# Two transformer layers on one core: the keys' transposition, a feed-forward product and its GELU move to other slots, two products change bank, and the routing bias is added in groups

## The chip, the core and the metric

The kernel runs on one core of a Trainium2 chip. A core has four compute engines that the text calls by the profile's names: PE (TensorE, matrix products; PEld is its weight load), DVE (VectorE), ACT (ScalarE) and POOL (GpSimd), and a queue engine SP that only starts transfers. Each engine executes its own list of instructions strictly in the order in which they were written; they wait for each other through semaphores. PE writes its results into eight PSUM banks, from which ACT and DVE read them. The metric is the device time of one execution in microseconds, the median over runs.

## The reference

Inputs are `x` (16 batches of 128 tokens, 128 wide) and a context of 77 tokens for each batch. Two layers follow each other:

```
x = x + tanh(g_xattn[0]) * L0_xattn(ctx, layernorm(x))   # 16 heads of 64, 77 context + 128 latent keys, masked softmax
x = x + tanh(g_ffn[0])   * L0_ffn(layernorm(x))          # 128 -> 512, butterfly, gelu, butterfly, 512 -> 128
x = x + tanh(g_xattn[1]) * L1_xattn(layernorm(x), ctx)   # 16 heads of 8, softmax over the 32 largest of 77 scores
x = x + tanh(g_ffn[1])   * L1_ffn(layernorm(x))          # router, one of 8 experts for each token
```

with, in the last of them,

```
route = sigmoid(x @ Wr + br)
max_prob, max_ind = max(route), argmax(route)
out = gelu(x @ W1[max_ind]) @ W2[max_ind] * max_prob
```

The 32 largest scores are found with four rounds of "the eight largest" and "replace them" for each head; this is the bulk of DVE's work.

## The kernel before

**Staging.** The 16 batches go through a software pipeline in `run_steps`. In a step `i` six batches are in the works: `P = i` (its keys are being normalised), `A = i-1` (first attention), `A2 = i-2` (end of the first attention, first feed-forward product), `B = i-3` (second feed-forward product, scores of the second attention), `C = i-4` (the 32 largest, softmax) and `E = i-5` (end of the second attention, router). Steps 0 to 5 and 16 to 20 are written out; steps 6 to 15 are one loop body that runs ten times. A step has eight slots; each engine has a function `step` that lists, slot by slot, what it issues. That list alone sets the order: there is no planner. After the last step the tokens are sorted by expert and the expert products run (the last 68 us); nothing in that stage is touched.

**The banks.** The eight banks are `GZ`, `S0`, `S1`, `TC`, `TL`, `OA`, `X`, `M`. `S0` and `S1` hold the first attention's scores, `TC` and `TL` its transposed probabilities, `GZ` and `OA` take turns for the projections, `X` holds 512-wide products (first feed-forward product, second attention's scores and transposed probabilities), and `M` everything small. Before PE writes a bank again it waits, in `free(name)`, for the semaphore of the last reader of that bank.

**The work around the change.** `keys_T` turns the normalised context and latents into bank `M`; `keys_out` on ACT copies them to `kvT`, which every projection of the batch needs. `queries_in`, `keys_in` and `values_in` are these projections; `queries_kept`, `keys_kept` and `values_kept` their copies on ACT; `scores(b, q)` are the scores of four heads; `maxima` on DVE the row maxima of two heads each; `exps(b, p)` the exponentials of two heads on ACT, which wait for the maxima; `normalise` on POOL, `probs_T` on PE, `probs_out` on ACT and `attend` on PE follow. `hidden` is the first feed-forward product (L892), `gelus` its activation on ACT (L1183, output `f_h`), `down` the second product (L900). `logits` is the router's product (L964), 8 columns wide. ACT needs another function table for Gelu than for Exp: the compiler puts an `ACT_TABLE_LOAD` in front of the first instruction that needs the other table. `top_32(b, k)` on DVE works on two heads; 8 of them belong to a batch.

In slot 0 before the change PE issues `keys_T(A)`, `attend(A2, GZ, 2)`, `down(B)` into `M`, the queries, the keys and `scores(A, 0)`; in slot 6 `hidden(A2)`; ACT issues `keys_out(A)` first in slot 0 and `gelus(A2)` in slot 6, ahead of `exps(A, 6)`; DVE adds the router's bias in slot 7 straight from bank `M`, and the residual of `down(B)` at the start of slot 0.

## Time and profile before

| | us |
|---|---|
| median of 3 runs | 811.86 (810.77 to 813.05) |
| the profiled execution | 816.19 |
| its span, from first to last instruction | 814.50 |
| PE busy in the span | 671.9 |
| DVE busy | 563.6 |
| ACT busy | 484.5 |
| POOL busy | 448.6 |
| ten passes of the loop body | 396.93 |

The span can be cut at the copy of `kvT` on ACT, of which there is one in each step. The steps from the sixth copy on (217.82 us) are alike in their work: 276 matmul records, 31.4 us of DVE and 28.3 us of ACT each. Their lengths are not all alike: in the ten loop passes there are lengths of about 38.7 and of about 40.3 us. The rows below come from one short and one long pass, and from the last step.

### The profile page before, as it was taken

What the parts mean: (1) busy time and instruction counts of PE and PEld (TensorE: products, weight loads), DVE (VectorE), ACT (ScalarE), POOL (GpSimd) and SP (SyncE); (2) the same over time, 40 slices, a digit from 0 to 9 for tenths busy, and PEclk for the clock granted to TensorE, in tenths of its full rate; (3) what the DMA queues carried; (4) which work ended last, traced back from release to release, by engine and by line L of the source; (5) the groups of instructions that cost most, each with busy time, mean ns of one, the idle gap of its engine ahead of it and who ended that gap; (6) DMA issues with size and microseconds to landing.
All of it is one profiled execution on the core that took longest, in us unless ns stands there. A gap on an engine that the chain in (4) does not pass through costs nothing.

```text
span 814.5 us, 19311 instructions
## 1 busy us (share of the span) xinstructions
PE 671.9 (82%) x4994; PEld 538.8 (66%) x4994; DVE 563.6 (69%) x3753; ACT 484.5 (59%) x1315; POOL 448.6 (55%) x689
## 2 busy tenths in 40 slices
PE   5498977889898989898989898989898968854696
PEld 4466665767676767667676767777767656543696
DVE  3266415778796969786868787878787889994232
ACT  1166558586767777777776776767776744221231
POOL 6445737565665646473737473737465553753144
PEclk9789999999999999999999999999999985555798
DMA  7200199900000000000000000000000000100672
GB/s 192 60 1 1 37 307 314 304 24 1 2 2 1 0 0 0 0 0 0 0 0 0 0 0 0 0 0 0 0 0 2 1 2 1 40 33 33 194 230 78
DMA packets 38535, 37.88 MB, mean 47 GB/s; under 512 B 3633, under 2 KB 34249, under 8 KB 38484
## 3 DMA queue, kind: packets, MB, share of 16 engines
q1 hardware_dynamic: 32986, 27.76, 12.0%
q10 hardware_dynamic: 3994, 6.36, 2.9%
q0 software_dynamic: 1504, 3.17, 1.1%
q8 instruction: 22, 0.36, 0.2%
q14 instruction: 29, 0.24, 0.1%
HBM read 16.28 MB, written 21.45 MB: 46 GB/s over the span
## 4 chain that ended last, share of the span: by engine, by line
PE 33%; ACT 21%; DVE 15%; issue 13%; POOL 11%; SPq 3%; DMA 2%; POOLq 1%; another core or an unknown queue 0%; DVEq 0%; ACTq 0%
DVE sw L1554 5%; ACT L1183 5%; PE bank L714 4%; ACT prob L1183 4%; PE bank L802 4%; DVE m L1548 4%; ACT sw L1183 3%; PE score_banks L844 3%; PE bank L900 3%; PE bank L1155 3%; POOL second_keys L496 3%; PE bank L814 3%; PE bank L1165 3%; PE bank L868 2%; PE bank L824 2%
## 5 line engine op out<-in xcount | busy, mean ns | idle before, releaser
L1554 DVE MATCH_REPLACE8 sw<-m,sw 128x77 f32<-128x77 f32 x1024 | 220.2, 222 | 0.0
L1548 DVE MAX8 m<-sw 128x8 f32<-128x77 f32 x1024 | 189.3, 226 | 8.7 <-DVE sw L1554 5.1
L1183 ACT ACTIVATE prob<-score_banks,negmax 128x205 f32<-128x205 f32 x256 | 108.2, 433 | 50.2 <-DVE negmax L1496 50.1
L503 POOL TENSOR_TENSOR sw<-sw,m 128x616 f32<-128x616 f32 x64 | 78.0, 1218 | 95.2 <-DVEq L1530 95.1
L484 POOL TENSOR_TENSOR prob<-prob,inv 128x820 f32<-128x820 f32 x64 | 99.4, 1554 | 50.6 <-DVE inv L1501 50.6
L1496 DVE TENSOR_REDUCE negmax<-score_banks 128x2 f32<-128x410 f32 x128 | 68.5, 577 | 62.1 <-PE score_banks L844 62.1
L937 PEld LDWEIGHTS bank<-v,p1T 77*128 77x128 f32 x512 | 73.8, 217 | 34.6 <-issue 20.6
L937 PE MATMUL bank<-v,p1T 77*128 (+1 forms) x512 | 74.5, 273 | 17.2 <-DVE rows_out L1508 12.6
L1554 DVE MATCH_VALUE_LOAD sw<-m,sw 128x8 f32 x1024 | 77.9, 76 | 0.0
L714 PEld LDWEIGHTS bank<-ident,prob 128*77 128x77 f32 (+1 forms) x512 | 57.5, 147 | 19.2 <-issue 18.8
L868 PE MATMUL bank<-ptc,z_ring 77*64 77x128 f32 x512 | 53.5, 284 | 20.0 <-ACT z_ring L1183 18.4
L714 PE MATMUL bank<-ident,prob 128*77 128x128 f32 (+1 forms) x512 | 68.0, 276 | 0.0
L824 PE MATMUL bank<-raw,kvT 128*128 128x512 f32 (+1 forms) x128 | 66.5, 602 | 0.0
L1183 ACT ACTIVATE h_ring<-bank 128x256 f32<-128x256 f32 (+1 forms) x87 | 38.6, 443 | 45.8 <-PE bank L1155 33.0
L1183 ACT ACTIVATE z_ring<-bank 77x512 f32<-77x512 f32 x64 | 38.1, 596 | 44.7 <-PE bank L824 44.6
L814 PE MATMUL bank<-kvT,raw 128*128 128x205 f32 x256 | 58.5, 353 | 0.8 <-ACT z_ring L1183 0.8
L844 PE MATMUL score_banks<-k_sb,q_sb 64*128 64x205 f32 x512 | 59.1, 348 | 0.0
L920 PE MATMUL bank<-second_keys,b_q 128*128 128x308 f32 x128 | 52.6, 495 | 4.7 <-ACT p1T L1183 4.7
L868 PEld LDWEIGHTS bank<-ptc,z_ring 77*64 77x64 f32 x512 | 29.9, 135 | 39.2 <-issue 39.1
L510 POOL TENSOR_TENSOR p<-sw 128x308 f32<-128x308 f32 x64 | 46.9, 733 | 15.8 <-ACT sw L1183 15.7
L1183 ACT ACT_TABLE_LOAD x34 | 43.6, 1283 | 19.8 <-issue 17.4
L1183 ACT ACTIVATE sw<-bank 128x308 f32<-128x308 f32 x64 | 28.1, 439 | 42.2 <-PE bank L920 42.2
(234 smaller groups left out, 1508.1 us busy)
## 6 DMA issues: line engine op xcount, KB each, us to landing
z_sorted<-no_row SPq DMA_DIRECT2D x1, 17415.0 KB, 62.9
raw<-in_L_ffn_W ACTq DMA_DIRECT2D x23, 256.0 KB
z_ring<-z_sorted SPq DMA_DIRECT2D x23, 129.0 KB, 3.5
w<-in_L_ffn_W SPq DMA_DIRECT2D x8, 256.0 KB, 4.2
raw<-in_L_xattn_Wkv SPq DMA_DIRECT2D x2, 512.0 KB, 10.8
xs<-in_x SPq DMA_DIRECT2D x1, 960.0 KB, 6.9
cx<-in_ctx SPq DMA_DIRECT2D x1, 577.5 KB
raw<-in_L_xattn_Wq SPq DMA_DIRECT2D x1, 512.0 KB, 10.6
```

The lines of the kernel that those rows point to most:

```text
L484: g.tensor_tensor(p, p, inv[:, 4 * q:4 * q + 4].unsqueeze(2).to_broadcast([128, 4, KV]), ALU.mult).then_inc(s["p_norm"], 1)
L503: g.tensor_tensor(v, v, m8[:, 4 * q:4 * q + 4, 0, 0:1].to_broadcast([128, 4, 2 * NK]), ALU.subtract).then_inc(s["sub_done"], 1)
L714: return nc.tensor.transpose(dst, src, ident[0:rows, 0:rows])
L814: last = mm(dst[:, KV * c:KV * c + KV], wkv_in[:, at:at + 128], kvT[:, :], start=True, stop=True)
L824: mm(dst[0:nr, :], kvT[:, r0:r0 + nr], wkv_in[:, INNER + 512 * j:INNER + 512 * j + 512], start=True, stop=True)\
L844: last = mm(SC[:, u, KV * r:KV * r + KV], q_sb[rows[u], q // 2, 2 * (q % 2) + r, :], k_sb[rows[u], q % 2, r, :], start=False, stop=(r == 1 ...
L868: last = mm(dst[64 * u:64 * u + 64, 128 * c:128 * c + 128], v[:, DH * h:DH * h + DH], p[:, 2 * c + u, :], start=not last_part, stop=last_p ...
L937: last = mm(M[:, c:c + D1 + 1], p1T[:, n, :], v1[:, bass.ds(b, 1), 4 * q + n, :].squeeze(1), start=True, stop=True)
L1183: return nc.scalar.activation(dst, src, f, **kw)
L1496: v.tensor_reduce(negmax[:, 2 * p:2 * p + 2], SC[:, :, KV * (p % 2):KV * (p % 2) + KV], AX_X, ALU.max, negate=True).then_inc(s["max_ready" ...
L1548: v.max(m8[:, h, r, :], sw[:, h, src, :]).then_inc(s[name], 1)
L1554: v.match_replace(sw[:, h, 1, :], m8[:, h, r, :], sw[:, h, src, :], TAKEN)\
```

## The change

* `keys_T` of the next batch is issued at the end of slot 7 of the step before, and `keys_out` likewise; before, both stood at the start of slot 0.
* `hidden(A2)` moves from slot 6 to slot 7, ahead of `keys_T`; `gelus` moves from slot 6 to the start of slot 0 of the next step.
* `down(B)` moves from slot 0 to slot 1 and writes bank `OA` instead of `M`; `project_out` writes `GZ` instead of `OA`; the first keys go into `TL` instead of `GZ`, and the other projections and `attend` exchange `GZ` and `OA` to match. The second keys are issued in slot 0, ahead of the first scores; the last values in slot 6.
* On ACT `exps(A, 1)`, `exps(A, 3)` and `exps(A, 5)` are issued ahead of copies that stood before them.
* On DVE the residual of `down(B)` and its statistics move from slot 0 to slot 2; the residual of `E` goes ahead of the maxima in slot 4; two normalisations go behind the maxima instead of into the middle of a `top_32`.
* ACT copies the logits to `route` (`keep_logits`); DVE adds the bias three times, for 11, 4 and 1 batches (`route_biases`), instead of 16 times.

```diff
@@ POOL
                     if slot == 0:
-                        if B is not None:
-                            rsqrt(B, b_mv, b_rs, "b_stats", "b_eps", "brs_ready")
...
+                    if slot == 2:
+                        if B is not None:
+                            rsqrt(B, b_mv, b_rs, "b_stats", "b_eps", "brs_ready")
@@ PE
             def down(b):
-                free("M")
+                free("OA")
...
                     if slot == 0:
-                        if A is not None:
-                            keys_T(A)
                         if A2 is not None:
-                            attend(A2, "GZ", 2, 2, 10)
-                        if B is not None:
-                            down(B)
+                            attend(A2, "OA", 2, 2, 10)
                         if A is not None:
-                            queries_in(A, "OA", 0, 0)
-                            keys_in(A, "GZ", 0, 1)
+                            queries_in(A, "GZ", 0, 0)
+                            reach(pe, "pt_ready", A2, 3)
+                            keys_in(A, "TL", 0, 1)
                         if E is not None:
                             second_probs_T(E, 3, 5)
                         if A is not None:
+                            keys_in(A, "OA", 1, 2)
                             scores(A, 0, 2)
...
                     if slot == 3:
                         if A2 is not None:
                             project_out(A2)
                         if A is not None:
-                            values_in(A, "GZ", "lat", 0, 5)
-                        if E is not None:
-                            context_T(E)
+                            values_in(A, "OA", "lat", 0, 5)
+                        if B is not None:
+                            second_T(B)
                         if A is not None:
                             probs_T(A, 0)
                         if E is not None:
-                            second_out(E)
+                            context_T(E)
                         if A is not None:
-                            keys_in(A, "GZ", 2, 6)
+                            keys_in(A, "OA", 2, 6)
+                        if B is not None:
+                            queries(B)
                         if C is not None:
                             second_probs_T(C, 1, 4)
+                        if E is not None:
+                            second_out(E)
...
                     if slot == 6:
-                        if A2 is not None:
-                            hidden(A2)
+                            values_in(A, "GZ", "lat", 1, 9)
...
                     if slot == 7:
+                        if A2 is not None:
+                            hidden(A2)
+                        if P is not None:
+                            keys_T(P)
@@ ACT
+            def keep_logits(b):
+                reach(act, "lg_psum", b, 1)
+                copy(route[:, bass.ds(b, 1), :].squeeze(1), M[:, 0:NE]).then_inc(s["lg_ready"], 1)
...
                     if slot == 0:
-                        if A is not None:
-                            keys_out(A)
+                        if B is not None:
+                            gelus(B)
...
                         if A is not None:
+                            keys_kept(A, OA, 1, 2)
                             exps(A, 0)
...
                     if slot == 7:
...
+                        if P is not None:
+                            keys_out(P)
@@ DVE
+            def route_biases(n):
+
+                b0, b1 = ROUTES[n]
+                if n == 0:
+                    dve.wait_ge(s["ld_router"], 32)
+                dve.wait_ge(s["lg_ready"], b1)
+                r = route[:, b0:b1, :]
+                v.tensor_tensor(r, r, br[:, :].unsqueeze(1).to_broadcast([128, b1 - b0, NE]), ALU.add)\
+                    .then_inc(s["r_biased"], 1)
...
-                    if slot == 0 and B is not None:
+                    if slot == 2 and B is not None:
                         reach(dve, "y_psum", B, 1)
                         reach(dve, "xb_added", B, 1)
-                        residual(B, batch(xs, B), M[:, 0:D], 2, "x2_ready")
+                        residual(B, batch(xs, B), OA[:, 0:D], 2, "x2_ready")
```

**PE, from the last instructions of slot 7 over the loop's head.** `p_ctx` and `p_lat` are what `keys_T` turns, `f_zT,w_up` is `hidden`, `second_keys,b_q` are the second attention's scores. Before:

```order
L824 MATMUL bank<-raw,kvT 128x512 [waits kvt_ready,w_ready]
L920 MATMUL bank<-second_keys,b_q 128x308 [waits kbd_ready,q_ready,h_ready]
L255 UNCONDITIONAL_BRANCH
L255 ISA
L242 ISA [waits lg_ready]
L714 MATMUL bank<-ident,p_ctx 128x77 [waits p_step]
L714 MATMUL bank<-ident,p_lat 128x128
```

After:

```order
L920 MATMUL bank<-second_keys,b_q 128x308 [waits kbd_ready,q_ready,sc_ready]
L892 MATMUL bank<-f_zT,w_up 128x128 [waits fT_ready,sc_ready]
L892 MATMUL bank<-f_zT,w_up 128x128 x3
L714 MATMUL bank<-ident,p_ctx 128x77 [waits p_step,lg_ready]
L714 MATMUL bank<-ident,p_lat 128x128
L255 UNCONDITIONAL_BRANCH
L255 ISA
```

The transposition now stands ahead of the branch, but behind `hidden`, which waits for ACT's copy of the scores out of bank `X` (`sc_ready`).

**ACT, around the first exponentials of a loop step.** `p1T` and `k_sb` are copies of projections or probabilities, `prob` is `exps(A, 0)`. Before:

```order
L1183 ACTIVATE k_sb<-bank 128x410 [waits w_psum]
L242 ISA
L1183 ACTIVATE p1T<-bank 77x512 [waits p1T_psum]
L242 ISA
L242 ISA [waits max_ready]
L1183 ACTIVATE prob,rowsum<-score_banks,negmax 128x205 [waits pt_psum]
L1183 ACTIVATE prob,rowsum<-score_banks,negmax 128x205
```

After:

```order
L1184 ACTIVATE p1T<-bank 77x512 [waits p1T_psum]
L242 REGISTER_ALU
L1184 ACTIVATE k_sb<-bank 128x410 [waits w_psum]
L242 ISA
L242 ISA [waits max_ready]
L1184 ACT_TABLE_LOAD
L1184 ACTIVATE prob,rowsum<-score_banks,negmax 128x205 [waits pt_psum]
L1184 ACTIVATE prob,rowsum<-score_banks,negmax 128x205
```

The table load that brings Exp back now stands behind the wait for the maxima.

**ACT, the same table load in slot 6 of a loop step before the change.** `f_h` is `gelus(A2)`, the `prob` behind it `exps(A, 6)`:

```order
L1183 ACTIVATE h_ring<-bank 128x256 [waits z_psum]
L1183 ACT_TABLE_LOAD
L1183 ACTIVATE f_h<-bank,bias_cols 128x128 [waits h_psum]
L1183 ACTIVATE f_h<-bank,bias_cols 128x128 x3
L242 REGISTER_ALU
L1183 ACT_TABLE_LOAD [waits pt_psum]
L1183 ACTIVATE prob,rowsum<-score_banks,negmax 128x205 [waits max_ready]
```

There the load stood ahead of the wait for the maxima.

## Rows read from the trace of the kernel before

**Rows 1.** Busy time by stretch: bounds, length, PE, PEld, DVE, ACT, POOL, clock.
```profile
217.82:614.75 396.93, 351.49 (x2760) 280.42 (x2760) 313.73 (x2191) 283.12 (x781) 226.77 (x311) 0.97 0.00 0
416.27:456.62 40.35, 35.81 (x276) 28.69 (x276) 31.37 (x220) 28.31 (x80) 22.66 (x32) 0.96 0.00 0
456.62:495.34 38.72, 34.18 (x276) 27.08 (x276) 31.38 (x220) 28.32 (x80) 22.67 (x32) 1.00 0.00 0
```

**Rows 2.** The same view inside the long step, two stretches of 2 us.
```profile
416.00:418.00 2.00, 1.32 (x8) 1.32 (x9) 1.06 (x9) 0.90 (x3) 2.00 (x3) 0.82 0.00 0
418.00:420.00 2.00, 2.00 (x10) 2.00 (x10) 0.83 (x3) 0.04 (x1) 0.42 (x3) 0.50 0.00 0
```

**Rows 3.** Waits of the short step: who, for whom, us, times, longest.
```profile
DVE negmax L1496 <- PE score_banks L844: 3.4, 2, 2.3
```

**Rows 4.** Timeline, slots 6 and 7: start, us, engine, line, operation, [idle before].
```profile
487.60 1.28 ACT L1183 ACT_TABLE_LOAD   x1
488.63 1.08 DVE L1496 TENSOR_REDUCE negmax<-score_banks 128x2 f32<-128x410 f32 x2 [1.15 <-PE score_banks L844]
488.89 1.14 ACT L1183 ACTIVATE f_h<-bank,bias_cols 128x128 f32<-128x128 f32 x4
490.05 1.28 ACT L1183 ACT_TABLE_LOAD   x1
491.35 0.43 ACT L1183 ACTIVATE prob<-score_banks,negmax 128x205 f32<-128x205 f32 x1
494.42 0.44 ACT L1183 ACTIVATE sw<-bank 128x308 f32<-128x308 f32 x1
495.34 0.36 ACT L1183 ACTIVATE kvT<-bank 128x205 f32<-128x205 f32 x1
```

**Rows 5.** Timeline from the first scores on, slots 0 and 1.
```profile
460.72 0.24 PE L839 MATMUL score_banks<-mask_now,ones_rows 64*128 64x154 bf16 x2 [0.50 <-ACT k_sb L1183]
461.63 1.10 PE L714 MATMUL bank<-ident,prob 128*77 128x128 f32 x8
461.77 1.08 DVE L1496 TENSOR_REDUCE negmax<-score_banks 128x2 f32<-128x410 f32 x2 [2.28 <-PE score_banks L844]
462.96 0.43 ACT L1183 ACTIVATE prob<-score_banks,negmax 128x205 f32<-128x205 f32 x1 [2.12 <-DVE negmax L1496]
463.79 0.58 ACT L1183 ACTIVATE ptc<-bank 77x512 f32<-77x512 f32 x1
464.75 0.51 ACT L1183 ACTIVATE k_sb<-bank 128x410 f32<-128x410 f32 x1
```

**Rows 6.** Timeline, third and fourth scores, slots 4 and 6.
```profile
475.18 0.43 ACT L1183 ACTIVATE prob<-score_banks,negmax 128x205 f32<-128x205 f32 x1
476.39 0.24 PE L839 MATMUL score_banks<-mask_now,ones_rows 64*128 64x154 bf16 x2 [1.22 <-ACT prob L1183]
488.49 1.06 PE L937 MATMUL bank<-v,p1T 77*128 x8
```

**Rows 7.** Timeline of PE: the products that change place, one of each.
```profile
457.03 1.16 PE L900 MATMUL bank<-wd,f_h 128*128 128x128 f32 x8 [0.78 <-ACT kvT L1183]
458.92 0.86 PE L814 MATMUL bank<-kvT,raw 128*128 128x205 f32 x4
486.49 1.16 PE L892 MATMUL bank<-f_zT,w_up 128*128 128x128 f32 x8
489.40 0.37 PE L964 MATMUL bank<-wr,r_zT 128*128 128x8 f32 x2
490.54 1.02 PE L824 MATMUL bank<-raw,kvT 128*128 128x512 f32 x2
492.71 0.28 PE L714 MATMUL bank<-ident,p_ctx 77*128 77x77 f32 x1 [0.62 <-DVE route L1659]
```

**Rows 8.** Timeline of the last step: bias, then exponential of the last logits.
```profile
745.28 0.17 DVE L1659 TENSOR_TENSOR route<-bank,br 128x8 f32<-128x8 f32 x1 [0.90 <-PE bank L964]
745.48 0.21 ACT L1183 ACTIVATE route<-route 128x8 f32<-128x8 f32 x1 [0.95 <-DVE route L1659]
```

More of the change, by code:

```diff
@@ L1107, in step @@
                         if A is not None:
-                            attend(A, "GZ", 1, 1, 6)
+                            attend(A, "OA", 1, 1, 6)
+                            values_in(A, "GZ", "lat", 1, 9)
+                        if E is not None:
+                            if i == 5:
+                                pe.wait_ge(s["ld_router"], 32)
+                            logits(E)
+                        if A is not None:
+                            scores(A, 3, 9)
+                        if C is not None:
+                            contexts(C, 2)
+                    if slot == 7:
+                        if A is not None:
+                            probs_T(A, 2)
+                        if B is not None:
+                            second_scores(B, 3)
                         if A2 is not None:
@@ L1313, in step @@
                         if A2 is not None:
-                            attended(A2, OA, 3)
+                            attended(A2, GZ, 3)
+                        if C is not None:
+                            second_exps(C, 1)
+                        if A is not None:
+                            values_kept(A, OA, v_ctx, 0, 4)
+                            exps(A, 2)
+                    if slot == 3:
+                        if A is not None:
+                            values_kept(A, OA, v_lat, 0, 5)
+                            exps(A, 3)
                         if B is not None:
@@ L1678, in between @@
                             normal(E, last_x(E), r_z, c_mv, c_rs, "crs_ready", "rz_ready")
+                    if A is not None:
+                        normals()
+                    if slot == 1 and E is not None:
+                        context_out(E)
+                    if slot in (1, 3, 7):
+                        close_top()
+                    def between():
+                        if A is None:
+                            normals()
                         if slot == 3 and A2 is not None:
```

161 lines of the change are left out of this document (64 added, 97 removed).

## The prediction

> **What bounds the kernel now.** I read busy time by step first. The ten passes of the loop take 396.93 us of the 814.50 us span, 39.69 us each [rows 1]. In a short pass of 38.72 us PE has 34.2 us of work, DVE 31.4 and ACT 28.3, so no engine is full: the step is as long as the chain that runs from engine to engine through it. The reader is to see a second thing in the same rows: the long pass has the same 276 matmuls and the same DVE and ACT time, but PE's time is 35.8 us and its mean granted clock 0.96 instead of 1.00. Inside the long pass the clock is 0.50, that is 1.2 GHz, from before 418 to 420 us and a little beyond, just behind a stretch in which PE was busy for 1.32 of 2 us [rows 2]. One such fall costs 40.35 - 38.72 = 1.63 us. With ten passes at 38.72 us the loop would take 387.2 us; it takes 9.7 us more, which is six falls in ten passes.
>
> Next the timeline, for who holds whom at the seam between two steps. In slot 6 ACT loads Gelu's table, computes GELU, loads Exp's table, and only then issues `exps(A, 6)` at 491.35, although the maxima were ready at 488.63 + 1.08 = 489.71: 1.64 us late [rows 4]. Then `keys_T` waits 0.62 us because DVE adds the routing bias late and only that frees bank M [rows 7]; `kvT` is copied at 495.34 [rows 4], the second feed-forward product waits 0.78 us for it [rows 7], and from one copy to the first scores it takes 460.72 - 456.62 = 4.10 us [rows 1, 5]. DVE stands 2.28 us there for the scores, out of 3.4 us that it waits for scores in the whole step [rows 3, 5].
>
> I count the step from the end of the first scores on PE (461.63, where the transposition of probabilities begins [rows 5]) to the same place one step later.
>
> **The change, part by part.**
>
> *First exponentials.* The maxima start 0.14 us after the first scores and `exps(A, 0)` at 462.96, 1.33 us after them [rows 5]. In the loop body Exp's table load now stands behind the wait for the maxima (the second pair of orders above), so its 1.28 us [rows 4] come in full: `exps(A, 0)` begins at 1.33 + 1.28 + 0.05 = 2.66. The pair takes 0.83, the two copies behind it 0.96 [rows 5], so `exps(A, 1)` begins at 4.45. From the start of such a pair to the scores that wait for it 476.39 - 475.18 = 1.21 us pass [rows 6]; the second scores begin at 5.66. What PE has to do until then is now a transposition, contexts, queries, another transposition and `down`, about 4.3 us by rows of their kind. PE waits 1.36 us where before it had no wait. In the trace the second scores followed `attend(A2, 3)` without a gap, so the lower bound is 0 (the load hidden), the upper 1.36; I take 1.36, because the order leaves nothing that hides it. The second waits and copies that `exps(A, 1)` was put ahead of (two copies, about 1 us) are already counted as gone.
>
> *Hand-overs between PE and ACT in slots 2 to 5.* `exps(A, 3)` now comes ahead of four copies, so the 1.22 us that PE waited for it before the third scores [rows 6] go. But the copy of the transposed second-attention input (`b_zT`) and the one of `f_zT` now stand behind a pair of exponentials (0.83 us each), and bank M passes in turn through `second_T`, `context_T`, `queries` and `second_out`, each of which waits for ACT's copy of the one before. Following both lists by hand I get about 0.65, 0.4, 0.15, 0.25, 0.5 and 0.2 us of waits, 2.15 in all, against about 2.0 before (the 1.22 and three small ones). I take +0.1. Below: only the 1.22 go and nothing comes, -1.2. Above: nothing goes and two pairs of exponentials come, +1.7.
>
> *Work moved in the stretch up to the fourth scores.* In come `down` (1.16), the last values (1.02) and the logits (0.37); out go the second keys (0.86) and `hidden` (1.16) [rows 7]: +0.5, of which I take +0.4, since neighbouring products overlap by a tenth or so. The fourth scores, which ended at 488.49 [rows 6], 26.86 after the start, so end 1.36 + 0.1 + 0.4 = 1.9 us later.
>
> *From the fourth scores to `kvT`.* Before, 495.34 - 488.49 = 6.85 us. Now the exponentials start right behind the maxima (-1.64) and the copy of the last values is gone (-0.5), but `kvT` is now behind `hidden`: that waits for the copy of the scores out of bank X, which before started 0.92 us ahead of the `kvT` copy, and takes 0.44 [rows 4], then 1.1 for `hidden` and 0.4 for `keys_T`. Sum: 1.34 to the maxima's end and its signal, 0.83 + 0.96 + 0.81 for exponentials and copies, 0.44, 1.1, 0.4 = 5.9. That is -0.95. So the transposition, though it stands ahead of the loop's branch, gives only a microsecond; PE stands idle for some 1.9 us ahead of `hidden`.
>
> *From `kvT` to the first scores.* ACT: the copy 0.36, table 1.28, four GELUs 1.14, `attended` 0.3, queries 0.5, keys 0.52, and 0.39 from the end of a keys' copy to the scores [rows 4, 5]: 4.5 us against 4.10, +0.4. Both removed waits, 0.62 and 0.78, lie inside these two stretches; what ends last there is no longer the bias or `kvT` but ACT's table load and GELU.
>
> *Sum of a clean step:* 1.9 - 0.95 + 0.4 = +1.3 us, 40.0 against 38.72. DVE has slack enough: its work falls by one addition (0.17 [rows 8]) and about 31.2 us plus some 2 us of hops fit in 40; the residual of `down`, moved behind two `top_32`, is read about 0.7 us before PE wants bank OA again. POOL moves with it and waits for DVE all the same.
>
> *The clock.* Before, 0.97 us per pass on average. The waits at the seam (0.6, 0.8 and 0.8 us) become one of 1.9 us, so a fall remains likely; it then lies over `hidden`, `keys_T` and `attend`, of which ACT's table load hides a part. I take six falls in ten at 1.0 us: 0.6 per pass, so -0.37. The Trainium skill ("TensorE: Matmul & The Clock Gate", Part 1) says that the gate is open only after recent activity and closes when PE idles; by that rule filling the seam would save up to 0.97 us per pass, the one joined wait saves nothing.
>
> *Other steps.* In steps 3, 4, 5 and 16, which are written out, the load stands ahead of the wait for the maxima: about 1.2 us less than in the loop, so nothing either way (0, between -1 and +1 each). In the last five steps DVE no longer waits for `down` in slot 0, -1; at the very end the logits go through one more copy, about 0.21 plus 0.05, before bias and exponential [rows 8], +0.3. Three grouped additions cost 0.6 once, beside other work.
>
> *The table load's price.* Here the trace shows 1.28 us and the next operation 0.01 us behind it, as in 488.89 after 487.60 [rows 4]. The Trainium skill ("ScalarE: Activation LUTs", What ACT_TABLE_LOAD costs) adds a drain and puts a switch at about 2.66 us. By that the first exponentials would come another 1.4 us late and the step be 41.4; the trace does not bear it out.
>
> **Sum.** Ten passes at +1.3 - 0.37 = +0.9 give +9; the rest gives -0.7, and I round down to +7 for the small overlaps that I counted in full. Against the profiled execution (816.19, of which 814.50 is span) that is 823; against the median of 811.86, which lies 0.5% under that execution, 819 us.
>
> **Rivals.**
>
> 1. *Faster: the hand-overs run at their lower bound and the clock stays up.* If only the 1.22 us go and nothing comes, the clean step is 1.36 - 1.2 + 0.4 - 0.95 + 0.4 = +0.0; with the falls gone (-0.97) each pass is 1 us shorter: 812 - 10 = 802. It decides from where PE's waits in slots 2 to 5 stay under some 0.9 us in all: then the fourth scores come no later than before. For it: the bias and `kvT` waits go, and DVE is far from full. Against it: the bank M chain and the 1.9 us wait. Chance 0.31.
>
> 2. *No change: loads and falls cancel.* Clean step +0.9 and no falls: 812 +- 2. For it: the uncertainty of the walk is as large as the gain. Chance 0.14.
>
> 3. *Slower still: every pass falls.* If the joined wait closes the gate in all ten passes at the present price of 1.63, the pass is 1.3 + 1.63 - 0.97 = +2.0, 832. For it: the one wait is about as long as the three of the present seam together. Against it: now, too, three or four passes in ten get by. Chance 0.10.
>
> 4. *The forecast,* slower by about 1 us a pass: 819. Chance 0.45.
>
> **How the numbers follow.** Less than 0.3%, 2.4 us, is what a measurement of this kernel can't tell from no change. Faster 0.31, same 0.14, slower 0.10 + 0.45 = 0.55. The range reaches from 801 (a little under rival 1) to 829 (short of rival 3's 832); what is outside are a gain of over 11 us and a fall in every pass. The forecast's own range is 814.5 to 826.
>
> **What would show it.** In the changed kernel's trace: (a) in a loop pass ACT_TABLE_LOAD between the maxima and `exps(A, 0)`, and PE idle 1 to 1.5 us before the second scores; in step 5 neither; (b) `exps(A, 6)` within 0.2 us of the maxima; (c) PE idle about 1.9 us ahead of `hidden`, released by ACT's copy `sw`; (d) waits of PE for `b_zT`, `c_zT` and `f_zT` copies, and none of over 0.5 us for `exps(A, 3)`; (e) clean passes of about 40 us at clock 1.00 and six of ten with a fall. Clean passes under 38.7, no wait before the second scores, or a clock of 1.00 in all ten would make the forecast wrong.

## The result, and the profile after

| us | before | changed |
|---|---|---|
| median | 812.45 (4 runs, 810.77 to 814.45) | 824.79 (4 runs, 821.80 to 828.23) |
| ratio | | 1.0152, 95% interval 1.0102 to 1.0202 |
| the profiled execution, its span | 816.19, 814.50 | 828.23, 826.50 |
| the same kernel, measured and profiled again later (e12) | 814.50 (28 runs) | 821.56 (7 runs), span 817.4 |
| ratio | | 1.0090, 95% interval 1.0062 to 1.0118 |

The change makes the kernel slower, by 0.9 to 1.5%. The profiled execution of the changed kernel was the slowest of its four, so I read a second one (e12 below) beside it wherever lengths matter. Busy time by stretch of the changed kernel: bounds, length, busy time of PE, PEld, DVE, ACT and POOL with instruction counts, granted clock. These rows answer to [rows 1].

```profile
212.91:616.93 404.02, 354.02 (x2759) 277.44 (x2756) 311.92 (x2183) 284.31 (x791) 225.75 (x311) 0.98 0.00 0
293.54:333.43 39.89, 34.70 (x281) 27.02 (x278) 31.18 (x220) 28.23 (x80) 22.54 (x32) 1.00 0.00 0
534.49:576.78 42.29, 37.62 (x284) 30.02 (x284) 31.16 (x220) 28.70 (x80) 22.57 (x32) 0.93 0.00 0
```

The reader is to see three things. The ten passes take 7.1 us more than before. A pass at clock 1.00 takes 39.89 instead of 38.72. And a pass in which the clock falls can cost more than one fall did before: the pass from 534.49, through which the clock stays at 0.50 (1.2 GHz) until 540.6, is 2.40 us longer than the clean one, against 1.63 in [rows 1].

What PE waits for in a clean pass (who, for whom, us in total, times, longest), in the kernel before (the short pass of [rows 1]) and then in the changed one:

```profile
PE score_banks L839 <- ACT prob L1183: 1.2, 1, 1.2
PE bank L900 <- ACT kvT L1183: 0.8, 1, 0.8
PE bank L868 <- ACT z_ring L1183: 0.8, 1, 0.8
PE bank L714 <- DVE route L1659: 0.6, 1, 0.6
PE score_banks L839 <- ACT k_sb L1183: 0.5, 1, 0.5
PE bank L937 <- DVE rows_out L1508: 0.4, 1, 0.4
PE bank L920 <- ACT p1T L1183: 0.2, 1, 0.2
```
```profile
PE bank L892 <- ACT sw L1184: 1.8, 1, 1.8
PE score_banks L839 <- ACT prob L1184: 1.3, 1, 1.3
PE bank L714 <- ACT b_zT L1184: 0.7, 1, 0.7
PE bank L714 <- ACT f_zT L1184: 0.5, 1, 0.5
PE bank L714 <- ACT f_h L1184: 0.5, 1, 0.5
PE bank L920 <- ACT p1T L1184: 0.3, 2, 0.2
```

The first changed row is the joined wait ahead of `hidden`, the second the one before the second scores. The waits are 4.5 us in all before and 5.1 after. The timeline of the changed pass (start, us, engine, line, operation, idle before) shows how the second comes about; it answers to [rows 5]:

```profile
297.88 0.24 PE L839 MATMUL score_banks<-mask_now,ones_rows 64*128 64x154 bf16 x2
298.92 1.08 DVE L1502 TENSOR_REDUCE negmax<-score_banks 128x2 f32<-128x410 f32 x2 [4.11 <-PE score_banks L844]
300.10 1.28 ACT L1184 ACT_TABLE_LOAD   x1 [1.74 <-DVE negmax L1502]
301.40 0.43 ACT L1184 ACTIVATE prob<-score_banks,negmax 128x205 f32<-128x205 f32 x1
304.26 0.24 PE L839 MATMUL score_banks<-mask_now,ones_rows 64*128 64x154 bf16 x2 [1.26 <-ACT prob L1184]
327.53 1.08 DVE L1502 TENSOR_REDUCE negmax<-score_banks 128x2 f32<-128x410 f32 x2 [2.40 <-PE score_banks L844]
328.64 0.43 ACT L1184 ACTIVATE prob<-score_banks,negmax 128x205 f32<-128x205 f32 x1 [1.52 <-DVE negmax L1502]
333.43 0.33 ACT L1184 ACTIVATE kvT<-bank 128x205 f32<-128x205 f32 x1
```

ACT was idle for 1.74 us and loaded the table only when the maxima were there (300.10), so `exps(A, 0)` starts at 301.40. `exps(A, 6)` starts at 328.64, 0.03 us after the maxima's end, where before it came 1.64 late.

**Where the 12.0 us of span went.** Cut at the sixth and the last copy of `kvT`, at the last maxima (before 648.08, after 650.95) and at the tile map (before 753.77, after 763.21):

| us, changed minus before | this execution | e12 |
|---|---|---|
| start to the sixth `kvT` (217.82 before) | -4.9 | -6.2 |
| ten passes (396.93 before) | +7.1 | +2.7 |
| to the last maxima (33.33 before) | +0.7 | +0.9 |
| to the tile map (105.69 before) | +6.6 | +4.5 |
| expert products to the end (60.7 before) | +2.6 | +0.9 |
| span | +12.0 | +2.9 |

The expert products have no changed instruction, and their difference was not pursued. The second column is less than the medians differ (7 us) because single executions are compared: the one of before took 816.19 us, 1.7 above its later median, and that of e12 took 819.18, 2.4 below its own.

In the ten passes two terms work against each other. In e12 the clean pass costs 10 x 1.15 = 11.5 us more, and the falls of the clock 1.0 us in all instead of 9.7; in the first execution these are 11.7, and 5.1 instead of 9.7.

I had forecast the second line and put next to nothing on the first and the fourth. They are large, and of opposite sign. The early steps, kernel before and then changed:

```profile
70.72:106.33 35.61, 29.38 (x224) 20.98 (x221) 17.58 (x53) 22.18 (x65) 21.57 (x29) 1.00 0.19 56
106.33:142.33 36.00, 29.63 (x234) 23.01 (x230) 14.63 (x84) 23.99 (x71) 20.97 (x29) 0.95 1.09 315
142.33:179.36 37.03, 31.64 (x258) 25.12 (x258) 29.43 (x217) 27.00 (x77) 22.02 (x29) 1.00 0.65 182
179.36:217.82 38.46, 34.18 (x276) 27.07 (x276) 31.42 (x220) 28.32 (x80) 22.74 (x32) 1.00 0.00 1
```
```profile
67.47:99.36 31.89, 29.74 (x228) 21.13 (x226) 17.38 (x53) 18.39 (x60) 22.00 (x29) 1.00 0.14 40
99.36:133.51 34.15, 27.75 (x226) 20.77 (x223) 16.34 (x85) 23.80 (x72) 20.91 (x29) 1.00 1.10 312
133.51:171.75 38.24, 32.13 (x262) 24.76 (x260) 29.41 (x213) 27.37 (x76) 21.55 (x29) 1.00 0.77 213
171.75:212.91 41.16, 36.36 (x280) 28.37 (x278) 31.00 (x220) 28.34 (x81) 22.61 (x32) 0.96 0.00 1
```

The first row of each pair differs by 3.72 us, and ACT's time (the fourth number) by 3.79: two table loads and the first batch's GELU have left this step for the next one. The rows are steps 2 to 5: the change gains 3.72 and 1.85 us in the first two and loses 1.21 and 2.70 in the others, of which the clock has a part (0.95 before in the second row, 0.96 after in the fourth). That is -1.66 in all. The other 3.25 us of the -4.9 lie ahead of these rows (70.72 against 67.47), where neither kernel has a GELU yet; no run separates what brings them.

The tail, cut at the context rows `c_z`; two of its stretches before, then changed:

```profile
662.12:693.29 31.17, 25.19 (x109) 20.95 (x109) 27.75 (x211) 11.28 (x23) 14.42 (x19) 0.57 0.01 2
693.29:718.38 25.09, 19.43 (x65) 14.04 (x65) 24.25 (x200) 7.97 (x17) 19.17 (x21) 0.50 0.13 48
```
```profile
665.97:699.63 33.66, 24.72 (x126) 19.86 (x126) 27.61 (x210) 12.37 (x25) 14.43 (x19) 0.65 0.02 5
699.63:728.76 29.13, 20.36 (x74) 16.02 (x74) 27.43 (x202) 9.06 (x18) 20.18 (x23) 0.50 0.11 38
```

In the tail DVE has few gaps (24.25 of 25.09 us busy in the second row), so what makes DVE late makes the step late. The second row grows by 4.04 us, and DVE's busy time there by 3.18: `b_z`, which stood in the row before, is 2.38 of it, and the residual of `down` with its statistics 0.81. The timeline of the changed kernel shows an instruction that became long:

```profile
705.50 2.38 DVE L1527 TENSOR_SCALAR b_z<-xs,b_mv,b_rs 128x128 f32<-128x128 f32 x1
705.53 2.26 POOL L496 TENSOR_TENSOR second_keys<-k1T,head_mask 128x1232 f32<-128x1232 f32 x1
708.02 0.45 PE L714 MATMUL bank<-ident,b_z 128*128 128x128 f32 x1 [4.54 <-DVE b_z L1527]
```

Before, the same two stood apart (`b_z` at 691.37 took 0.33 us, POOL's spreading of the keys began at 696.51). Now `b_z` lasts 2.05 us longer; it begins while POOL's previous instruction still runs (704.84 to 705.56) and ends 0.09 us behind the end of the spreading, and PE waits 4.54 us for it in all. DVE's `MAX8` beside POOL keeps its length (0.37). The Trainium skill ("SBUF — State Buffer", SBUF: two separate sides) says that GpSimd and a DVE instruction of certain kinds (in a 2-port mode, or with two SBUF inputs) lock a shared port pair against each other, and that the one that starts first has it for its whole instruction. The rows fit that, since POOL was at work first; why POOL's next instruction went ahead of `b_z` too is open, and no run shows in which mode `b_z` ran.

The same happens in every loop pass, on a smaller scale. In the changed loop `b_z` stands beside another multiplication of POOL's, of 0.74 us (308.31), and takes 0.75 us (308.38) instead of 0.34; no wait of PE's is for it. Before, it was the normalisation `r_z` that met this multiplication and took 0.88 us (323.38), and 0.39 after the change, so that DVE's busy time comes out even.

### The profile page after: what moved, and what is told of

It is laid out like the page before. It is cut to its first block, busy times and chain, and to the rows that moved or that the text cites. A ratio compares the mean times of both kernels' runs of the same rounds, so it can differ in the third digit from the quotient of the medians.

```text
span 826.5 us, 19323 instructions
## 1 busy us (share of the span) xinstructions
PE 677.7 (82%) x4994; PEld 536.7 (65%) x4994; DVE 566.5 (69%) x3740; ACT 487.0 (59%) x1331; POOL 448.0 (54%) x689
## 4 chain that ended last, share of the span: by engine, by line
PE 38%; DVE 16%; issue 16%; ACT 14%; POOL 10%; SPq 2%; DMA 2%; POOLq 1%; another core or an unknown queue 0%; DVEq 0%; ACTq 0%
DVE sw L1560 6%; PE bank L868 5%; DVE m L1554 4%; PE bank L824 4%; PE bank L714 4%; PE score_banks L844 4%; ACT prob L1184 4%; PE bank L937 3%; PE bank L814 3%; PE bank L920 3%; PE bank L1156 3%; ACT L1184 2%; PE bank L1166 2%; DVE negmax L1502 2%; POOL sw L503 2%
## 5 line engine op out<-in xcount | busy, mean ns | idle before, releaser
L937 PEld LDWEIGHTS bank<-v,p1T 77*128 77x128 f32 x512 | 71.8, 217 | 24.9 <-issue 12.0
L824 PE MATMUL bank<-raw,kvT 128*128 128x512 f32 (+1 forms) x128 | 68.3, 615 | 1.9 <-DVE xs L1514 1.9
L868 PE MATMUL bank<-ptc,z_ring 77*64 77x128 f32 x512 | 55.9, 297 | 1.9 <-issue 1.9
L1184 ACT ACTIVATE sw<-sw 128x616 f32<-128x616 f32 x64 | 45.5, 711 | 19.9 <-POOL sw L503 19.8
L714 PE MATMUL bank<-ident,p 128*77 128x128 f32 x256 | 45.5, 306 | 10.1 <-ACT f_h L1184 8.3
L868 PE MATMUL bank<-ptl,z_ring 128*64 128x128 f32 x512 | 53.3, 287 | 0.0
```

The costliest lines, as they stand in the source:

```text
L714: return nc.tensor.transpose(dst, src, ident[0:rows, 0:rows])
L824: mm(dst[0:nr, :], kvT[:, r0:r0 + nr], wkv_in[:, INNER + 512 * j:INNER + 512 * j + 512], start=True, stop=True)\
L868: last = mm(dst[64 * u:64 * u + 64, 128 * c:128 * c + 128], v[:, DH * h:DH * h + DH], p[:, 2 * c + u, :], start=not last_part, stop=last_p ...
L937: last = mm(M[:, c:c + D1 + 1], p1T[:, n, :], v1[:, bass.ds(b, 1), 4 * q + n, :].squeeze(1), start=True, stop=True)
L1184: return nc.scalar.activation(dst, src, f, **kw)
```

## The experiments

Medians of the kernel before, measured at different times, drift by a microsecond or two, so the ratio to the kernel before, measured in turn on the same chip, is what counts. "Clean pass" is the shortest of the ten loop passes in the trace of the run; in all runs but e2 its clock is 1.00. Four kernels ran together each time: e1 to e4, e5 to e8, e9 to e12.

| | ratio, 95% interval | clean pass | ten passes | last maxima to tile map |
|---|---|---|---|---|
| before | 1 | 38.71 | 396.93 | 105.69 |
| changed | 1.0152 (1.0102 to 1.0202) | 39.89 | 404.02 | 112.26 |
| e12, changed again | 1.0090 (1.0062 to 1.0118) | 39.87 | 399.67 | 110.18 |
| e1, Exp's table early | 1.0079 (1.0047 to 1.0110) | 39.55 | 398.54 | 109.99 |
| e2, GELU in slot 6 | 1.0250 (1.0218 to 1.0281) | none (40.34 at clock 0.96) | 408.67 | 106.07 |
| e3, bias alone | 1.0043 (1.0021 to 1.0064) | 38.85 | 399.97 | 103.50 |
| e4, old tail | 1.0086 (1.0056 to 1.0117) | 39.87 | 400.34 | 108.90 |
| e5, exponentials back | 1.0229 (1.0190 to 1.0268) | 39.81 | 411.07 | 110.27 |
| e6, transposition alone | 0.9992 (0.9976 to 1.0009) | 38.70 | 396.79 | 102.85 |
| e7, transposition first | 1.0070 (1.0048 to 1.0093) | 39.87 | 399.44 | 111.89 |
| e8, four edits | 1.0212 (1.0175 to 1.0249) | 40.84 | 408.84 | 106.89 |
| e9, exps(A, 3) alone | 1.0014 (0.9990 to 1.0039) | 38.72 | 404.32 | 103.80 |
| e10, early steps alone | 0.9988 (0.9953 to 1.0022) | 38.67 | 399.68 | 102.90 |
| e11, changed, mended | 0.9985 (0.9961 to 1.0010) | 39.56 | 401.56 | 106.95 |

Five traces of kernels with the tail of before (before, e3, e6, e9, e10) give 102.85 to 105.69 from the last maxima to the map; the trace of before is the longest of them because DVE there stood for 3.13 us on one wait that takes 1.05 in the others. So the changed tail, 110.18 and 112.26 us, costs 6 to 9 us, more than the 4.5 to 6.6 of the table above. The profiled execution of e9 was by far its longest (826.25 against a median of 815.36), with three passes of 43.0 us, so its ten passes are not compared.

**e1: is the exposed table load what the loop lost?**

```
+                            if i is None:
+                                fn(scr[:, :], tg[:, 0:1], ACT.Exp)
                             exps(A, 0)
```

> The changed kernel plus one instruction: in the loop body ACT computes an exponential of one unused column into a scratch column just before it waits for the first maxima, so that Exp's table load stands ahead of that wait; nothing else moves. Theory A (the load behind the wait is what PE waits for before the second scores): the 1.26 us gap before the second scores in a clean loop pass goes, exps(A, 0) begins 0.05 us behind the maxima, a clean pass falls from 39.9 to 38.7 to 38.9 us, ten passes from 404.0 to about 393, the whole from 825 to about 814. Rival B (the step's length is set by DVE's and ACT's work around the seam, and the gap only moves): PE's wait shows up before the third scores or before hidden, clean pass 39.5 or more, whole above 820.

The mechanism did what it should, and the time did not follow. ACT of e1:

```profile
337.45 1.28 ACT L1185 ACT_TABLE_LOAD   x1
338.75 0.20 ACT L1185 ACTIVATE scr<-tg 128x1 f32<-128x1 f32 x1
339.19 0.43 ACT L1185 ACTIVATE prob<-score_banks,negmax 128x205 f32<-128x205 f32 x1 [0.24 <-DVE negmax L1505]
```

and what PE waits for in that clean pass:

```profile
PE bank L893 <- ACT sw L1185: 1.8, 1, 1.8
PE bank L715 <- ACT b_zT L1185: 0.7, 1, 0.7
PE bank L715 <- ACT f_zT L1185: 0.7, 1, 0.7
PE bank L825 <- DVE xs L1517: 0.6, 1, 0.6
PE bank L715 <- ACT f_h L1185: 0.5, 1, 0.5
```

The 1.3 us are gone; 0.6 us for DVE's residual of `down`, which frees bank `OA` for the values, and 0.2 more for `f_zT` have come. The pass is 0.34 us shorter: most of the exposed load was cover for the next wait. The numbers are rival B's, though the wait has come back at another place than it named. As a whole e1 (1.0079) is not told apart from the changed kernel in e12 (1.0090), whose interval overlaps.

**e2: GELU and `hidden` back in slot 6.**

```
                     if slot == 6:
+                        if A2 is not None:
+                            hidden(A2)          # PE; gelus(A2) likewise on ACT
                     if slot == 7:
-                            hidden(A2)
```

> The changed kernel with the first feed-forward product and GELU put back into slot 6 in every step, all else as changed. Theory A (moving GELU by one seam takes two table loads and 1.1 us of GELU out of the third step, which is where the early gain of 4 us comes from, and puts them into step 18, where the tail loses): the written-out steps 2 to 5 lose about 3 us, the tail gains 3 to 5 us, a loop pass gets exps(A, 6) 1.6 us late again (+1.6) but first scores 2.4 us earlier and no exposed Exp load before the second scores (-1.3): clean pass 38.5 to 39.0, whole 810 to 815. Rival B (the other hand-overs cost the loop its 1.2 us): clean pass stays 39.5 to 40, whole 820 to 826.

Theory A holds for the tail and for step 2. Step 2 takes 34.51 us instead of 31.89 at nearly the same clock (0.99 and 1.00), 2.6 more. Steps 3 to 5 take 36.95, 40.96 and 42.70 us, but at a clock of 0.92 each, so that their 2.8, 2.7 and 1.5 us are not the move's alone. The contexts `c_z` of step 18 come 29.6 us after those of step 17 instead of 33.66 (32.08 in e12), and the tail is 4 to 6 us shorter.

The loop takes 408.67 us, and most of that is the clock: the granted clock is 0.96 in every one of the ten passes, and ten falls at the 0.80 us that one costs the changed kernel (my estimate) are 8 of the 9.8 us above ten clean changed passes. A typical pass, and the longest of PE's waits in it:

```profile
304.36:345.48 41.12, 36.13 (x276) 28.41 (x276) 30.74 (x216) 28.54 (x81) 22.22 (x32) 0.96 0.00 0
```
```profile
PE bank L937 <- ACT route L1184: 1.4, 1, 1.4
PE bank L802 <- ACT kvT L1184: 0.7, 1, 0.7
```

PE's waits are 4.9 us in all, no more than the 5.1 of the changed kernel's clean pass; PE's busy time is 36.13 us instead of 34.70, which is the longer pass. In slot 6 GELU stands ahead of the copy of the logits, which now frees bank `M` for the contexts, and that makes the wait of 1.4 us; but the waits of 1.8 and 1.3 us are gone for it. A changed pass with a fall takes 40.68 us at the same 0.96 (212.91:253.59), so at equal clock e2's passes, 40.87 on average, are 0.2 us longer. No pass of e2 is at full clock, so neither theory's clean pass was put to the test. Nor is it one unlucky execution: all four of e2 took 834.3 to 834.8 us, with a mean granted clock of 0.891 to 0.901, against 0.910 to 0.924 in e12's seven. In the changed arrangement the move of GELU pays, for the most part through the clock; what it would do by itself in the kernel before is not shown.

**e3 and e6: two parts alone, in the kernel before.** e3 copies the logits on ACT behind `exps(A, 6)` and adds the bias in groups; e6 moves the transposition of keys and its copy to the end of the step before.

```
-                        v.tensor_tensor(batch(route, E), M[:, 0:NE], br[:, :], ALU.add)      # e3
+                            keep_logits(E)                                                   # e3, ACT, slot 6
-                            keys_T(A)         # e6, slot 0
+                            keys_T(P)         # e6, slot 7
```

> The kernel before with the routing bias alone changed: ACT copies the logits out of bank M behind exps(A, 6), DVE adds the bias to 11, 4 and 1 blocks in three additions. Theory A: the 0.62 us that the transposition of keys waits for DVE's addition in each pass goes, and what ends last there is ACT's copy of kvT behind its own queue, so 0 to 0.3 us per pass and a clock fall fewer: whole 808 to 812, -1 to -4 us against before. Rival B: the extra 0.2 us copy on ACT stands in its chain behind exps(A, 6) and delays kvT: +2 us.

> The kernel before with the transposition of the next block's keys and its copy alone moved to the end of the step before (the routing bias is still added per block, which holds bank M for 0.6 us). Theory A (the transposition itself was never late by more than its two waits, 0.6 for the bias and 0.8 before down): it goes 0.5 us earlier and down's wait for kvT goes, clean pass 38.0 to 38.6, whole 807 to 812. Rival B (PE then holds the transposition behind the fourth second scores, and ACT's copy of it stands behind the second exponentials, so that nothing comes earlier): clean pass 38.7 to 39.2, whole 812 to 818.

e3 is slower by 3.5 us at the median; its clean pass is 38.85, and the wait for the bias has turned into 0.4 us for ACT's copy and 0.3 us more for the last values' copy, which stands behind it: rival B. e6 is the kernel before: a clean pass of 38.70, and the same waits of the same length (0.8 for `kvT`, 0.6 for the bias). Neither theory's gain came. The place of the transposition, ahead of the branch or behind it, is worth nothing while what it waits for stays.

**e5 and e7: two parts undone, in the changed kernel.** e5 puts the three exponentials back behind the copies; e7 issues the transposition ahead of `hidden`.

```
                             values_kept(A, OA, v_lat, 0, 5)
-                            exps(A, 3)        # e5; 1 and 5 likewise
...
                             keys_kept(A, OA, 2, 6)
+                            exps(A, 3)
```
```
+                            keys_T(P)         # e7, slot 7
                             hidden(A2)
-                            keys_T(P)
```

> The changed kernel with exps(A, 1), exps(A, 3) and exps(A, 5) put back behind the copies on ACT that they stood behind before; nothing else. Theory A (putting exponentials ahead of copies was neutral in the loop: it took away PE's 1.2 us before the third scores and brought 0.7 for b_zT, 0.5 for f_zT and 0.3 for p1T): clean pass within 0.4 us of 39.9, the waits for b_zT and f_zT go and one of about 1.2 us for exps(A, 3) comes back, whole 822 to 828. Rival B (the new order of ACT is what costs the loop): clean pass 39.0 or less, whole under 817.

> The changed kernel with the transposition of keys ahead of hidden in slot 7 on PE, nothing else. Theory A (PE stands 1.8 us ahead of hidden for ACT's copy of the scores, and kvT stands behind both): kvT is copied about 1.2 us earlier in the step, hidden fills PE's wait for the copy of kvT, the wait for sw shrinks, and queries and first scores come earlier: clean pass 38.8 to 39.2, whole 813 to 817. Rival B (GELU, which needs hidden, is what ends last before the first scores, since its copies stand behind it on ACT): clean pass 39.7 to 40, whole 822 to 826.

e5's clean pass is 39.81: neutral, as theory A has it (its waits are 1.8, 1.7, 0.6, 0.5, 0.3, 0.2). Yet the run is 6 to 11 us slower than the changed kernel (by the ratios, 2.3% against 1.5 and 0.9%), and that is the clock, which no theory had: 411.07 - 10 x 39.81 = 13.0 us of the ten passes. All four executions of e5 have a mean granted clock of 0.899 to 0.905, and those of e7 on the same chip 0.918 to 0.923. Two passes of e5 with the same work:

```profile
550.12:589.93 39.81, 34.58 (x281) 27.03 (x278) 31.27 (x220) 28.13 (x81) 22.62 (x32) 1.00 0.00 0
506.26:550.12 43.86, 39.15 (x282) 31.01 (x278) 31.47 (x220) 28.40 (x81) 22.60 (x32) 0.88 0.00 0
```

Three of its ten passes are like the second, 4.05 us longer, with DVE and ACT as busy as in the first. There are two falls in it: the clock is 0.50 at its start, until about 509.6, and again from 520.1 to 526.6, and 1.00 between and behind them. In e7 the clean pass stays at 39.87 (rival B: the wait ahead of `hidden` is still 1.6 us); all ten passes are clean but one, which is 0.6 us longer.

**e4 and e8: the tail.** e4 gives steps 17 to 20 the slots of before, and puts GELU and `hidden` into slot 6 from step 16 on. e8 does so for batch B's work from step 18 and for GELU from step 17, and has three edits in the loop as well.

```
+                late = i is not None and i >= 17         # e8, e11: 18
-                    if slot == 2 and B is not None:
+                    if slot == (0 if late else 2) and B is not None:     # residual, b_z; down, rsqrt, second_T likewise
```

> The changed kernel with the order of before in the steps behind the loop: down, its residual, rsqrt and b_z in slot 0, second_T in slot 2, queries behind contexts(C, 0) in steps 17 to 20, hidden and GELU in slot 6 of steps 16 and 17; loop and early steps as changed. Theory A (the tail's loss of 8 to 9 us comes of this order: GELU and its two table loads ahead of the copy that the contexts wait for, and b_z beside the spreading of keys): last c_z comes 7 to 9 us earlier, whole 816 to 818. Rival B (the tail is late because of the route bias and the copy of the logits, or because its clock is at half): under 3 us, whole 822 or more.

> The changed kernel with four edits at once, each readable at its own place in the trace: Exp's table loaded ahead of the wait for the first maxima in the loop; keys' transposition ahead of hidden; the residual of down inside the top-32 of slot 1 on DVE, so that bank OA is free for the values (0.6 us of PE's waits in the run with the early load); and in the tail GELU of step 17 in slot 6 and, from step 18, block B's products, residual and b_z in the slots of before. Theory A: clean pass 39.9 - 0.35 - 1.0 - 0.5 = 38.0 us, tail from the last maxima to the tile map 112.3 -> about 105 us (4.0 of it between the c_z of steps 18 and 19), whole 795 to 803, faster than before. Rival B (the step is as long as PE's work, 34.7 us, and waits that only change places): clean pass over 39, whole 810 or more.

The stretch of step 18's work, the second tail row above, in e4:

```profile
695.69:720.83 25.14, 18.96 (x63) 13.86 (x64) 24.23 (x199) 7.17 (x16) 19.12 (x21) 0.50 0.14 49
```

It is 25.1 us as before, against 29.13 in the changed kernel, and 25.14 too in e11, which has e8's tail: 4.0 us are shown to be batch B's order in step 18, with `b_z` beside the spreading of the keys (in e4 it takes 0.34 us again). GELU has no part in it, since e2 has 29.12. Which part of B's order does it (the place of `b_z` or the later residual) was not separated. The rest of the theory fails: e4 pays 17.06 us from the last maxima to the first `c_z` instead of 15.02 (14.51 in e12), where step 16 now computes GELU twice, and its tail as a whole is only 3.4 us shorter (1.3 against e12's).

e8's loop is slower, 40.84 us a pass against 39.56 in e11, which differs from it only in the place of the residual. The collision of the tail is now in the loop:

```profile
311.73 2.25 POOL L497 TENSOR_TENSOR second_keys<-k1T,head_mask 128x1232 f32<-128x1232 f32 x1
311.81 2.25 DVE L1553 TENSOR_SCALAR b_z<-xs,b_mv,b_rs 128x128 f32 x1
```

With the residual inside the top-32, `b_z` follows POOL's spreading of the keys by 0.08 us and takes 2.25 us instead of 0.75, in all ten passes (2.25 to 2.28). DVE is busy 32.52 us a pass instead of 31.15; PE waits 1.0 us for `b_z` itself and 1.1 for DVE's rows ahead of the contexts. All ten passes of e8 are at clock 1.00.

**e9: the hand-over alone, in the kernel before.**

```
                             queries_out(B)
+                            exps(A, 3)        # was behind keys_kept(A, GZ, 2, 6)
```

> The kernel before with exps(A, 3) alone moved up on ACT, from behind the copy of the third keys to right behind queries_out, where ACT stood idle for 1.06 us. Theory A (a hand-over pays where the exponentials fill ACT's idle time and nothing that PE waits for stands behind them): PE's 1.22 us before the third scores fall to about 0.3, clean pass 38.72 -> 37.9, whole 804 to 808. Rival B (as in the changed kernel, the copies behind it come late and the waits only change places): PE waits as long for the copies of the values, of c_zT or of the keys, clean pass 38.5 or more, whole 811 or more.

The 1.22 us before the third scores of [rows 6] are gone, and the clean pass is 38.72, as in [rows 1]. The longest of what PE waits for now:

```profile
PE bank L937 <- DVE rows_out L1509: 1.4, 1, 1.4
PE bank L868 <- ACT z_ring L1183: 0.8, 1, 0.8
```

Before, the first row had 0.4. The time has moved to the next place where PE meets DVE. DVE's four maxima stand 7.5, 8.8 and 10.6 us apart in both kernels, and it waits for neither the second nor the third: there DVE's list sets the pace, and PE's wait was slack. The numbers are rival B's, but the wait is for DVE, which it did not name.

**e10 and e11: is there a better kernel?** e10 takes the changed order in steps 0 to 3 only, and is e9 from step 4 on. e11 is the changed kernel with e1's load, e7's swap and e8's tail.

```
+                if i is not None and i <= 3:      # e10, on each engine
+                    return early_step(i, at)
```

> The order of the changed kernel in steps 0 to 3 only, and the kernel before with exps(A, 3) moved up (the edit of e9) from step 4 on; step 4 computes GELU twice. Theory A (the changed order is worth 8.8 us by the seam of steps 3 and 4, because there the loads and GELU stand where ACT is idle, and costs time only in full steps and in the tail): the seam stays 8 us earlier, step 4 gives 2 to 3 us back for the second GELU, and the whole is 5 to 6 us faster than e9. Rival B (the early steps only run ahead of something that the later ones wait for anyway, the weights' preparation or the top-32): under 2 us between the two.

> The changed kernel with early load of Exp's table, keys' transposition ahead of hidden, and the tail's two edits of e8, but the residual of down in slot 2 as changed. Theory A (the residual inside slot 1's top-32 was what made e8 a microsecond longer per pass): clean pass 39.3 to 39.6, tail from last maxima to tile map about 107 us, whole 811 to 816. Rival B (the early load and the swap do it together): clean pass over 40.5, whole over 825.

> The changed kernel unaltered, on the same chip as the others, for a second trace of it. Both theories: 819 to 826, clean pass 39.9. If its falls come at other places and fewer, 399 to 401 us for the ten passes, 3 to 5 of the 7 us that the loop lost belong to the clock of one execution; if the same passes are long again, they belong to the program.

In e10 the seam of steps 3 and 4 comes at 134.71 instead of 142.33, and the sixth `kvT` at 213.21 instead of 217.82, so most of the early gain lasts; the run is 0.3% ahead of e9, which the intervals do not separate, and level with the kernel before. e11 mends what the change had cost (0.9% in e12, measured beside it) and is level too: 0.9985 (0.9961 to 1.0010), with its clean pass of 39.56. e12 says that most of the loop's long passes belonged to one execution: there one pass of ten is 0.80 us longer than the clean one, the rest within 0.05.

## Why the prediction was right, and where not

The forecast was slower, 819 us in a range of 801 to 829; measured were 824.8 and, later, 821.6.

- **First exponentials:** right. The load stands behind the maxima, `exps(A, 0)` begins 2.61 us after the transposition of probabilities (forecast 2.66), the second scores 5.47 after it (5.66), and PE waits 1.26 (1.36). In step 5, which is written out, the wait is absent, but there PE waits 0.9 us for the residual of `down` instead, as in e1. But the price of the wait is not its length: e1 took it away and got 0.34 us.
- **Hand-overs:** about right. `b_zT` 0.7 (0.65), `f_zT` 0.5 (0.5), no wait for `exps(A, 3)`; `c_zT` did not wait in the clean pass, against sign (d). In all PE waits 1.54 us between the second and the fourth scores (2.15 forecast), against 1.77 before (2.0), so -0.2 and not +0.1. e5 confirms the term from the other side, 39.81 against 39.89.
- **Up to the fourth scores:** forecast +1.9; from 298.79 to PE's next work behind the fourth scores at 327.38 are 28.59 us against 26.86, +1.73. **To `kvT`:** forecast 5.9 and -0.95; 6.05 us and -0.80, with 1.8 us ahead of `hidden` (1.9). **To the first scores:** forecast 4.5 and +0.4; 297.88 - 293.54 = 4.34, +0.24.
- **Clean pass:** forecast +1.3, measured 39.89 - 38.72 = +1.17, of which PE's waits are 0.6 (5.1 against 4.5) and its busy time 0.5.
- **The clock:** I forecast six falls in ten at 1.0 us, 0.6 per pass. The first execution has five falls in ten passes, which cost 404.02 - 10 x 39.89 = 5.1 us, 1.0 each; e12 has one, of 0.80 us. So the clock gave back 0.5 to 0.9 us per pass where I had 0.37. One price per fall is too simple: a fall costs 1.6 us in the kernel before, 0.80 where it lies over the start of a changed pass, and the one from 534.0 to 540.6 costs 2.4 us in its pass; the passes with 4.05 us more hold two. The number of falls goes with the order of the instructions as well: ten in ten passes in e2, none in e8.
- **Other steps, the failed term.** "The rest gives -0.7": steps 3 to 5 at nothing (between -1 and +1 each), the last five steps at -1. Measured were -4.9 (-6.2 in e12) before the loop (-3.25 ahead of step 2, -3.72 in step 2, then -1.85, +1.21 and +2.70 in steps 3 to 5) and 6 to 9 us behind it. I had walked through the full step alone. The seam that GELU was moved across is also the border between an empty step and one where ACT has slack, and between the last full step and one that has nothing to hide GELU behind; and in the tail `b_z`, which costs no wait of PE's in the loop, came to stand beside POOL's longest instruction of the step. The size of the tail's loss fits the two: 4.0 us for batch B's order (e4, e11) and 2.5 to 4 for GELU's place (e2). The early gain and the tail's loss cancelled to within a few microseconds. That the total lies so near the forecast is luck in these two terms, and not in the loop's.
- **Rivals.** The first rival's rule, that the fourth scores come no later if PE waits under 0.9 us in slots 2 to 5, counts waits of PE as time: in the changed kernel they are 1.54 us there, so it was not tested as it stands, but in e9 the 1.22 us went and the pass did not move.
- **The table load's price.** The trace of e1 has the load at 337.45 and the next activation at 338.75, 0.02 us behind its end, much as in [rows 4]. The Trainium skill ("ScalarE: Activation LUTs", What ACT_TABLE_LOAD costs) puts a switch at about 2.66 us; no run here shows the part beyond 1.28.

**What stays open.** The +1.17 us of the clean pass. Of the parts taken singly, the bias gives +0.13 (e3), the transposition -0.02 (e6), the exponentials' order 0.08 (e5) and the exposed load 0.34 (e1). What is left, some 0.6 us, is the place of `hidden` and GELU (e2 has no pass at full clock) together with PE's order and the banks in slots 0 to 3; that follows by elimination from parts measured in two different kernels, and no run tried it. Nor is it known why the clock falls once, twice or not at all in passes with the same work.

## What to carry to other kernels

When work is moved across a step's border in a software pipeline, walk through the first and the last steps as well as the full one: they lose and gain whole occurrences of it (here -5 us before the loop and at least +6 behind it, as much as the ten passes together). A wait in the profile is worth what is late behind it, not its length: of 1.26 us removed 0.34 came back, of 1.22 us removed nothing. When a DVE instruction changes place, look at which POOL instruction it then runs beside, in every kind of step. In a loop body, an activation on a spare column ahead of a wait brings the table load out from behind that wait.

## What the runs showed of the hardware

- A DVE scaling of 128x128 took 0.33 us alone, 0.75 us beside a POOL multiplication of 0.74 us, 2.25 us (e8) beside one of 2.25 us that had started 0.08 us earlier, and 2.38 us where one of 2.26 us followed another on POOL 0.03 us after the scaling's start.
- Passes with the same instructions and the same waits differed by up to 4.05 us through the granted clock alone (mean clock 0.88 against 1.00 over the pass, e5), and two executions of the same kernel spent 5.1 and 1.0 us in ten passes on it. Kernels that differ in the order of a few instructions had ten falls (e2) and none (e8) in ten passes. A comparison of single executions of this kernel is no finer than that; the shortest pass repeats to 0.02 us.
